# Batched attention and mixture kernel on one core: own buffers for attention outputs, merged mask pieces, condition rows in column groups, a new written order

## The reference, cut to what matters

```
ada = cond @ w_ada + b_ada                       # 6 rows of 256: shift, scale, gate, twice
x1  = mobius_add(x,  expmap(g1 * logmap(plin(attention(heads(plin(modulate(x)))))))   # 16 heads of 16, full 256 x 256 softmax
x2  = mobius_add(x1, expmap(g2 * logmap(plin(plin(modulate(x1), w_f1), w_f2))))
h   = x + (gate * local window attention(x2) + gate * attention to 64 pooled latents) @ w_out
z   = ((h * cond / 16) @ weight) * rsqrt(norm of cond * weight)
out = h + sum over the top 2 of 4 experts e: w_e * relu(z @ Wi' + (z @ A_e') @ B_e') @ Wo'
```

## Time and profile before

| | |
|---|---|
| median of 3 runs | 1249.25 us (1247.89 to 1251.9) |
| the profiled execution | 1248.74 us, its span 1246.9 us |
| mean granted TensorE clock | 0.978 |
| busy PE, DVE, ACT, POOL | 1158.8, 853.8, 706.5, 238.3 us |
| instructions | 34256 |

### The profile page before, as it was taken

One profiled execution on the slowest core, in us unless ns is written; L12 is line 12 of the kernel. 1 busy time (PEld: TensorE's weight loads), 2 busy tenths in 40 slices (PEclk: granted clock), 3 DMA queues, 4 the chain that ended last, 5 costly groups with the idle time before them and its releaser, 6 DMA issues.

```text
span 1246.9 us, 34256 instructions
## 1 busy us (share of the span) xinstructions
PE 1158.8 (93%) x13948; PEld 824.2 (66%) x13948; DVE 853.8 (68%) x3321; ACT 706.5 (57%) x1429; POOL 238.3 (19%) x336
## 2 busy tenths in 40 slices
PE   6977769999999999999999999999999999999996
PEld 2544445676667677767777677766777667777764
DVE  6858768886986857767677788767577785552332
ACT  1456676658766654757376755757465754434221
POOL 2302022022112210141113111041112120210111
PEclk9978889999999999999999999999999999999998
DMA  9220001000010100000010101000010000000000
GB/s 317 96 81 13 22 15 28 23 29 13 28 36 19 36 2 28 27 27 28 9 46 2 31 15 32 14 23 11 3 32 6 28 16 19 11 11 19 20 10 9
DMA packets 27231, 38.51 MB, mean 31 GB/s; under 512 B 3489, under 2 KB 21281, under 8 KB 27073
## 3 DMA queue, kind: packets, MB, share of 16 engines
q1 hardware_dynamic: 25280, 34.29, 8.6%
q10 hardware_dynamic: 1792, 2.03, 0.5%
HBM read 31.62 MB, written 4.29 MB: 29 GB/s over the span
## 4 chain that ended last, share of the span: by engine, by line
PE 74%; DVE 10%; ACT 9%; issue 4%; POOL 1%; DMA 1%; ACTq 0%; DVEq 0%; POOLq 0%
PE psg L436 44%; PE psq L436 16%; PE pso L436 7%; PE psg L439 7%; ACT PQ L1379 4%; DVE nm L929 2%; DMA QK<-in_w 1%; ACT QK L1379 1%; POOL M L1719 1%; ACT JA L1390 1%; DVE TU L926 1%; DVE lp L926 1%; ACT M L1379 1%; DVE JD L942 0%; DVE R L926 0%
## 5 line engine op out<-in xcount | busy, mean ns | idle before, releaser
L1379 ACT ACTIVATE PQ<-psq 128x2048 f32<-128x2048 f32 x112 | 210.2, 1877 | 86.0 <-PE psq L436 85.5
L1744 POOL TENSOR_TENSOR R<-R,rhoT 128x256 f32<-128x256 f32 x128 | 90.7, 729 | 429.0 <-ACT R L1379 429.0
L436 PE MATMUL psq<-QK 32*128 32x128 f32 (+5 forms) x3360 | 129.6, 303 | 0.2 <-DMA QK<-in_w 0.2
L436 PE MATMUL psg<-zT,WiT 128*128 128x256 f32 x512 | 123.8, 385 | 2.8 <-DVE R L926 2.7
L436 PE MATMUL pso<-PQ,Vg 128*32 128x256 f32 (+2 forms) x2048 | 111.3, 349 | 12.3 <-ACT PQ L1379 9.5
L436 PE MATMUL psg<-WoT,R 128*128 128x256 f32 x512 | 115.6, 381 | 0.0
L436 PEld LDWEIGHTS psq<-QK 32*128 32x128 f32 (+2 forms) x3360 | 93.0, 165 | 22.7 <-issue 13.7
L929 DVE TENSOR_REDUCE nm<-psq 128x16 f32<-128x2048 f32 (+1 forms) x48 | 92.7, 1931 | 21.8 <-PE psq L436 21.4
L436 PEld LDWEIGHTS psg<-zT,WiT 128*128 128x128 f32 x512 | 93.5, 192 | 18.3 <-DVE R L926 3.9
L436 PEld LDWEIGHTS psg<-WoT,R 128*128 128x128 f32 x512 | 95.2, 190 | 14.9 <-issue 2.6
L1379 ACT ACTIVATE R<-psg 128x512 f32<-128x512 f32 x64 | 38.1, 595 | 117.8 <-PE psg L436 117.6
(11 more groups left out here) (224 smaller groups left out, 2281.6 us busy)
## 6 DMA issues: line engine op xcount, KB each, us to landing
bcB<-ada_rows SPq DMA_DIRECT2D x16, 384.0 KB, 3.4
bcA<-ada_rows SPq DMA_DIRECT2D x15, 384.0 KB, 3.5
X<-in_x SPq DMA_DIRECT2D x16, 256.0 KB, 5.0
XR<-in_x SPq DMA_DIRECT2D x16, 256.0 KB, 2.7
out<-XR SPq DMA_DIRECT2D x16, 256.0 KB, 2.2
QK<-NMT SPq DMA_DIRECT2D x128, 3.0 KB
WiT<-in_WiT SPq DMA_DIRECT2D x1, 1024.0 KB, 4.9
WoT<-in_WoT SPq DMA_DIRECT2D x1, 1024.0 KB, 7.4
```

What stands on the lines that cost most here:

```text
L436: return e.matmul(o, lhsT, rhs, start=start, stop=stop, skip_group_check=True)
L1379: return e.activation(o, i, func, **kw)
L1744: e.tensor_tensor(R4, R4, rhoT[:, :], ALU.mult).then_inc(*pool_moe.mark(b, f"r{f}{j}"))
```

## The change

- O1 and OS are tiles of their own. ACT's copies of `heads(b)` wait for the last scores of batch b-1 in place of its OT.
- Local score turns: two score pieces of equal width stand side by side, and their mask is one instruction per tile with the mask row repeated. 32 mask instructions in a turn in place of 48.
- Condition rows: condT is padded to 32 columns; the three products go to partitions 0, 32 and 64 of psq[2]. DVE adds bias and the ones of the scale rows (from two new columns of hsel) in two operations of 96 partitions. The bias comes in three loads of 32 partitions. The three writes to DRAM wait for the second of these operations.
- `b1w`: 8 products in four column groups (`b1p`), an ACT copy to VB, then one product with a selecting column that sums the four groups. `b1b`: ACT squares b1 and sums along the row, then one product sums over partitions. `ff(0)` waits for the last condition row; `mix(0)` no longer does.
- hsel is loaded earlier; the written order of all five engines is new. On SP, x of batches 4 and 5 and both XR come before the late loads.

```
 "PE": [
-  "AA*AAn*qqqq*******hhn*qqqqa*naaaaaaaooohhoaqqaaqaaqaaaoonohohqNqqqFFaaaaaaaaooppopoppphhmaaaaaaaamoomNnm",
+  "A*An*qqqq****h*h**a***aanaaaaqaqooqqnohohqaqqaaqaanaahaqhooaqqaaqaoaoaaaaNhoohFFaaaoaaoaaaooppppppomomNmn",
...
 "SP": [
-  "n*****wAxwxxxAAnnN*nnNxnmNnxNnxmewNnxmNnewxmNnemwxNnxmewNnmewxNnmewNnmNewnmNewmewNmewNmNewmewmewmewee",
+  "nwxwx*****xxAAAnnN*nnNnxnmNxmNnexwnNmxNnewxmNnxmNewnxmewNnxmNewnmewNnmewNnmewNmewNmNewNmNewmewmewmewee",
...
-        O1, OS = ST1[:, 0:2], ST1[:, 2:4]
+        O1, OS = (sb(n, [128, 2, 256]) for n in ("O1", "OS"))
...
-        turns = [[(0, 0, 0), (0, 1, 192), (1, 0, 320)], [(1, 1, 0), (3, 1, 128)], [(2, 0, 0), (2, 1, 192), (3, 0, 320)]]
+        turns = [[(0, 0, 0), (1, 0, 192), (0, 1, 384)], [(1, 1, 0), (3, 1, 128)], [(2, 0, 0), (3, 0, 192), (2, 1, 384)]]
...
-                for j, o in enumerate((psq[0:16, 2, :], psq[0:16, 3, :], pso[0:16, :])):
-                    yield
-                    if j:
-                        for c in range(2):
-                            w.wait_ge(*loads[f"wada{c}1"])
-                    for c in range(2):
-                        last = mm(o, condT[:, c, :], wada[c][:, 512 * j:512 * j + 512], c == 0, c == 1)
-                    last.then_inc(*pe_ada.mark(0, f"r{j}"))
+                yield
+                for c in range(2):
+                    w.wait_ge(*loads[f"wada{c}1"])
+                for c in range(2):
+                    for j in range(3):
+                        last = mm(psq[32 * j:32 * j + 32, 2, :], condT[:, c, :], wada[c][:, 512 * j:512 * j + 512], c == 0, c == 1)
+                last.then_inc(*pe_ada.mark(0, "r"))
...
+                bank = take(pg, ("b1p",), act_late.at(0, "b1p"))
+                w.wait_ge(*loads["b1c"])
+                for h in range(2):
+                    for j in range(4):
+                        f = 4 * h + j
+                        last = mm(bank[32 * j:32 * j + 32, :], b1c[:, f:f + 1].broadcast_to([128, 32]), wx[h][:, j, :], h == 0,
+                                  h == 1)
+                last.then_inc(*pe_late.mark(0, "b1p"))
+                yield
                 bank = take(pg, ("b1w",), act_late.at(0, "b1x"))
-                w.wait_ge(*loads["b1c"])
-                for f in range(8):
-                    last = mm(bank[:, :], b1c[:, f:f + 1].broadcast_to([128, 128]), wx[f // 4][:, f % 4, :], f == 0, f == 7)
+                w.wait_ge(*loads["hsel"])
+                w.wait_ge(*act_late.at(0, "b1p"))
+                mm(bank[:, :], hsel[:, 3:4].broadcast_to([128, 128]), VB[:, :], True, True).then_inc(*pe_late.mark(0, "b1w"))
...
-                    for c, kt, q0 in turns[v]:
-                        n = 128 if kt else 192
-                        for i, j, r, o in tiles():
-                            m = 96 - 32 * j
-                            mm(psq[o, i, q0:q0 + n], unit(r), MK[r, m:m + n], q0 == 0, False)
-                    if v == 1:
-                        for i, j, r, o in tiles():
+                    n = 128 if v == 1 else 192
+                    for i, j, r, o in tiles():
+                        m = 96 - 32 * j
+                        mm(psq[o, i, 0:2 * n].rearrange("p (h n) -> p h n", h=2), unit(r),
+                           MK[r, m:m + n].unsqueeze(1).broadcast_to([32, 2, n]), True, False)
+                    for i, j, r, o in tiles():
+                        if v == 1:
                             m = 128 - 128 * (j % 2)
                             mm(psq[o, i, 256:512], unit(r), MLT[r, m:m + 256], False, False)
+                        else:
+                            m = 96 - 32 * j
+                            mm(psq[o, i, 384:512], unit(r), MK[r, m:m + 128], False, False)
...
-                for j, i in enumerate((psq[0:16, 2, :], psq[0:16, 3, :], pso[0:16, :])):
...
-                        stt(adaR[j][:, o], i[:, o], float(n in (1, 4)), bada[n // 3][0:16, k:k + 256], ALU.add,
-                            ALU.add)().then_inc(*s.mark(0, f"a{n}"))
+                for h in range(2):
+                    yield
+                    o = slice(256 * h, 256 * h + 256)
+                    w.wait_ge(*pe_ada.at(0, "r"))
+                    stt(adaR[:, o], psq[0:96, 2, o], hsel[0:96, 6 + h:7 + h], bada[1][:, o], ALU.add,
+                        ALU.add)().then_inc(*s.mark(0, f"a{h}"))
...
+                yield
+                w.wait_ge(*pe_late.at(0, "b1p"))
+                copy(VB[:, :], pg.where["b1p",][:, :]).then_inc(*s.mark(0, "b1p"))
+                e.activation(b1c, b1c, ACT.Square, accum_out=bb1[:, :]).then_inc(*s.mark(0, "b1q"))
...
                     if b:
-
-                        w.wait_ge(*pe_out.at(b - 1, "OT"))
+                        w.wait_ge(*pe_att.at(b - 1, "sc3"))
```

More of the change, by code:

```diff
@@ L47 @@
[L47 to L51, removed]
@@ L346, in program @@
         xr_in, out_done = [landing(f"d_xr{i}") for i in range(2)], [landing(f"d_out{i}") for i in range(2)]
-        pe_ada = sig("pe_ada", "bc", "r0", "r1", "r2")
-        dve_ada = sig("dve_ada", "c0", "c1", "c2", *[f"a{i}" for i in range(6)])
-        act_late = sig("act_late", "W0", "W1", "b1w", "b1x", "b1b")
+        pe_ada = sig("pe_ada", "bc", "r")
+        dve_ada = sig("dve_ada", "c0", "c1", "c2", "a0", "a1")
+        act_late = sig("act_late", "W0", "W1", "b1p", "b1q", "b1w", "b1x", "b1b")
         pool_setup = sig("pool_setup", "zero", "ones", "ident", "identb")
         pool_late = sig("pool_late", "mask", "wgkv", "gt0", "gt1", "w2sq")
-        pe_late = sig("pe_late", "W0", "W1", "b1w", "b1b", "w2sq")
+        pe_late = sig("pe_late", "W0", "W1", "b1p", "b1w", "b1b", "w2sq")
         dve_late = sig("dve_late", "gv0", "gv1", "g00", "g01", "g10", "g11", "ys", "yq", "dz", *rs("d"), "dT", "Bh", "Bl", "Bm", "Bst")
@@ L501, in late @@
                 yield
+                bank = take(pg, ("b1p",), act_late.at(0, "b1p"))
[7 more added lines that the diff above has]
+                yield
                 bank = take(pg, ("b1w",), act_late.at(0, "b1x"))
-                w.wait_ge(*loads["b1c"])
-                for f in range(8):
-                    last = mm(bank[:, :], b1c[:, f:f + 1].broadcast_to([128, 128]), wx[f // 4][:, f % 4, :], f == 0, f == 7)
-                last.then_inc(*pe_late.mark(0, "b1w"))
+                w.wait_ge(*loads["hsel"])
+                w.wait_ge(*act_late.at(0, "b1p"))
+                mm(bank[:, :], hsel[:, 3:4].broadcast_to([128, 128]), VB[:, :], True, True).then_inc(*pe_late.mark(0, "b1w"))
                 yield
                 bank = take(pg, ("b1b",), act_late.at(0, "b1b"))
-                for f in range(8):
-                    last = mm(bank[:, 0:2], b1c[:, f:f + 1].broadcast_to([128, 128]), b1c[:, f:f + 1].broadcast_to([128, 2]),
-                              f == 0, f == 7)
-                last.then_inc(*pe_late.mark(0, "b1b"))
+                w.wait_ge(*pool_setup.at(0, "ones"))
+                w.wait_ge(*act_late.at(0, "b1q"))
+                mm(bank[:, 0:2], bb1[:, :].broadcast_to([128, 128]), Vg1[:, 0, 0:2, 16], True, True
+                   ).then_inc(*pe_late.mark(0, "b1b"))
                 yield
@@ L990, in late @@
                 yq = lq[:, 3].rearrange("p (c b) -> p c b", c=2)
-                yield from chain(s, 0, ("ys", "yq"), ts(ysT[:, :, :], condT[:, :, :], 1.0 / 16, None, ALU.mult),
+                yield from chain(s, 0, ("ys", "yq"), ts(ysT[:, :, :], condT[:, :, 0:16], 1.0 / 16, None, ALU.mult),
                       tt(yq, ysT[:, :, :], ysT[:, :, :], ALU.mult))
@@ L1225, in ff @@
                         w.wait_ge(loads["adaA"][0], 32)
+                        w.wait_ge(*loads["adaB"])
                     w.wait_ge(*pe_ff.at(b, f"ug{t}"))
@@ L1282, in mix @@
                 bv = pg.where["rl", b][:, :].rearrange("p (h n) -> p h n", n=32)
-                w.wait_ge(*loads["adaB"])
                 w.wait_ge(*pe_mix.at(b, "rl"))
@@ L1401, in setup @@
                 load(e, "bqkv", bqkv[:, :], A["bqkv"].partition_broadcast(128))
-                load(e, "bada1", bada[1], A["b_ada"][768:1536].partition_broadcast(16))
+                for j in range(3):
+                    load(e, f"bada1{j}", bada[1][32 * j:32 * j + 32, :], A["b_ada"][512 * j:512 * j + 512].partition_broadcast(32))
                 load(e, "bo", bo[:, :], A["b_o"].partition_broadcast(128))
@@ L1767, in setup @@
                 load(e, "ident", ident0, A["ident"])
+                load(e, "hsel", hsel[:, :], A["hsel"])
                 load(e, "wqkv", wqkv[:, :, :], chunks("wqkv"))
@@ L1774, in setup @@
                 load(e, "w21", wx[1][:, :, 256:512], chunks("w2")[:, 4:8])
-                load(e, "hsel", hsel[:, :], A["hsel"])
                 for _ in x_load(2):
```

138 lines of the change are left out of this document (72 added, 66 removed).

## The result

The changed kernel takes 1233.49 us (median of 4 runs, 1232.33 to 1236.6) against 1248.76 us of the kernel before beside it (4 runs): ratio 0.9877, 95% interval [0.9852, 0.9902], 15.3 us less. Measured once more, as one of the second four experiments, it is 0.9858 [0.9835, 0.9881], 18.4 us less. The forecast was 20.5 less. The profiled execution took 1232.33 us with a span of 1230.2, so the spans differ by 16.7 us.

What follows compares the result with a forecast made beforehand. PE was taken to bound the kernel, save in the pipeline's filling, where batches wait on their own chains. Terms 14 + 3 + 5 - 1.5 = 20.5 us off 1248.7 gave 1228 us, range 1211 to 1242.

Steps and rivals of the forecast that it cites:

- Part 1: Condition and bias rows in the setup: column groups and fewer products save 9.3 us of PE (3.5, 4.2 and 1.6).
- Part 2: Order up to the first scores: they come at 44 us instead of 58, 14 us earlier, with DVE ending last.
- Part 3: O1/OS buffers and the filling, first scores to mixture: 3 us shorter; bounds 10 longer to 14 shorter.
- The bound of 14 us: Most the filling could shrink: 40 us of idle PE times 0.37, as missing time falls from 46 to 29.
- Part 4: Merged mask pieces, 48 to 32 instructions a turn: 0.105 us saved in each of 48 turns, 5.0 us.
- my upper bound: Most the merged masks could save: 10.1 us, if 32 instructions cost what 16 do.
- Part 5: Steady part and tail: little to gain, 13 us of tail idle stay; taken together 1.5 us lost.
- A: Rival: early start lost again because DVE and ACT set the filling, mixture only 3 us earlier; 1241 us, chance 0.17.
- B: Rival: filling shrinks 14 us and not 3, steady part keeps 2 more; 1215 us, chance 0.18.
- C: Rival: slower through the single score tile psq, 0.2 us less PE work between users adds 32 us; 1260, chance 0.07.
- D: Rival: no change, columns and not instructions price the masks, and A holds with nothing left; 1247 us, chance 0.08.
- The signs named: Trace checks: first scores at 44 (42 to 47), XR at 218, 2560 masks, 0.45 to 0.50 us a turn, steady PE 97%.

Runs made afterwards that it cites:

- second four experiments: Changed kernel again, and three variants of it or the kernel before (masks split, old order, own buffers alone), on one chip: ratios 0.9858, 0.9916, 0.9913, 1.0004.
- last experiment: Changed kernel with two letters of the written order moved, one on ACT and one on DVE: 1233.97 us, ratio 0.9867.
- second experiment: Kernel before with only the column groups for condition rows and the new bias rows; order fitted, masks and O1/OS as before: 1252.21 us, ratio 1.0001.
- third experiments: Changed kernel with the old written order, adapted only where steps fell away or came in: 1239.82 us, ratio 0.9903.

## Why the prediction was right, and where it was wrong

The direction, the size within 5 us and the range held, but by errors of opposite sign, so that the total came out near is in part luck. Against the span: start 15.9 for 14 (+1.9), filling -6.9 for +3 (-9.9), after it 7.7 for 5.0 - 1.5 (+4.2). That is 3.8 short of 20.5, the 16.7 measured.

**Part 1** held: 1.85 us for the condition rows (1.7 forecast), 2.8 for b1w (1.9 and 0.9), 0.14 for b1b. The condition rows lasted 2.10 in the second measurement and 2.95 in the last experiment, where the granted clock was lower. The square of w2c moved to 39.59 as expected, without holding anything up. That all this gives nothing in the old order was not said; the second experiment shows it.

**Part 2** held, and its numbers more closely than its sentence. "DVE, not PE, ends last there" is true of the old order once PE has less to do (3.50 us of wait in the second experiment) and half true of the new one: U came at 35.7 and not at 39, PE waited 1.53 for it and then worked without a gap until 42.01. Without that wait PE is ready at 40.5 (40 forecast).

**Part 3** is the step that failed: "I let it shrink by 3 us". The count of new PE work was right (116 to 126 us; busy time rose by 10.5). The stalls were over-valued: idle PE fell by 3.6 us and not by 13. The reasoning took a stall as removed when its place in the order was eased. But other waits took its place, which fits a chain through three engines (added work costs 9.9, 11.1 and 8.6 us for 10.2, 9.3 and 10.2). That the closing up of this chain is what ate the stalls is read from the timelines. (The bound of 14 us should be 15 by its own factors, 40 x 0.37; nothing hangs on it.) The profile also shows how the early start was spent. Batch 0's first product of ff stands at 121.54 where it stood at 121.88, although the first scores came 16 us earlier; the new order has 8 more attention steps in front of it (24 for 16). So 16 us were laid out for the other batches' attention, and 9 came back at XR. This reading rests on the timelines; no run moved batch 0 alone.

**Part 4** had the right mechanism at half its size: 0.212 us a turn (0.583 to 0.37) for 0.105. For 48 turns that is 10.2 us of PE, my upper bound. 45 turns lie behind the first XR transposes. PE's busy time there fell by 9.4 us in the old order (973.9 to 964.5) and the stretch by 7.3; in the new order, where two of three split turns hold PE 0.56 us, by 7.7 (970.8 to 963.2) and 6.9. The pair of the second and third experiments gives 9.4 (1013.6 to 1004.2), but its first value is 1.8 to 1.9 above the two other traces of the old masks in the old order. The fault was the straight line between 16 and 48 instructions: the cost of 32 is that of 16. The other price weighed there, one matmul plus 4 ns for each further tile of a pack (the Trainium skill, TensorE: Matmul & The Clock Gate, Measured speedup vs the span model), would have given 3.1 us and is further off: it had fitted the group of 16 and does not give the 0.21 us between 32 and 48.

**Part 5**: the 1.5 us of losses did not come. Behind XR the old and the new order take the same 1004 us; the added wait of ff(0) and the changes of tile shape cost nothing that shows.

**The rivals.** A (start lost, XR over 228, 1241): half of it happened. XR at 226.2 lies nearer to 228 than to my 218, and without the masks' full price the time would have been near A's. The reason given, DVE and ACT setting the filling, was nearer to the truth than my count of gaps; but 10 us more on PE cost as much. B (XR under 210) did not come: the stalls moved. C: PE's waits for PQ in front of scores grew from 10.8 to 15.2 us, 4.4 and not 32. D: columns alone don't price the masks, since with the same columns the masks alone give 0.95%.

**The signs named.** First scores within 42 to 47, yes, at its edge. XR at 218, no. 2560 mask instructions, yes; 0.45 to 0.50 us to the first score, no, 0.37. Clock of the filling over 0.88, yes, 0.90. PE at 97% in the steady part, yes. No idle of 5 us behind an Exp sequence, yes: the one of 5.88 us stands behind statistics. PE's waits for PQ past 10.8 were to prove me wrong, and they grew past it without doing so: 3.3 us of the 15.2 are one wait, at 55.71, where ACT loads the Ln table and the Exp table again (1.28 us each) between two Exps. The bound was set without a price.

## What to carry to other kernels

Before pricing an edit in a stretch where an engine is 75 to 80% busy, ask whether anything in it is covered: adding 10 us to each engine in turn tells a chain (all cost) from a bound (one does). Put the additions at more than one place, and read TensorE's busy time and granted clock beside them. As the timelines here read, in a chain a removed stall is worth only what is left when the next one has closed up, and an early start is worth what the first batch gets of it. Where the engine is full, as here behind the filling, most of the work taken off it comes back (6.9 of 7.7 us and 7.3 of 9.4), so a modest edit repeated 48 times was worth as much as the whole new order.

## What the runs showed of the hardware

**Mask packs: 32 instructions cost what 16 do, 48 cost more.** With 512 columns per tile of 32 x 32 in each case, 16 and 32 instructions hold PE 0.37 us and 48 hold it 0.58 (0.56 with pieces of 192, 192 and 128). Pieces of 384 and 128 columns cost what two of 256 do. With 256 columns per tile 32 instructions hold it only 0.27, in all 16 batches of the kernel before, so at 32 the columns still count:

```profile
1160.87 0.34 PE L436 MATMUL psq<-maskb,identb 32*32 32x128 bf16 x32
1161.14 1.13 PE L436 MATMUL psq<-QK 32*128 32x64 f32 x32
```

Why 48 cost 0.21 more was not tried.

**A late chain on DVE ran into POOL.** The first scores came at 41.7 to 43.3 us in seven executions with the new order's start, and at 46.05 in the kernel with two letters moved, both of them behind the first scores. There PE waited 2.78 us for U at 39.77. The chain was late before it met POOL: PE had waited 2.88 us for the load of w (1.75 in the changed kernel) and came back at the lower clock (0.55 between 15.9 and 22.6, where the changed kernel had 1.00 up to 20.0), and batch 0's qkv products stood at 24.80 for 22.00.

```profile
15.96 3.75 PE L437 MATMUL psq<-QK 128*128 128x512 f32 x4 [2.88 <-DMA QK<-in_w]
...
39.77 0.63 PE L440 MATMUL psg<-ident,U 128*128 128x128 f32 x4 [2.78 <-DVE U L935]
```

Just ahead of POOL's three products DVE was 2.0 us behind the changed kernel (hy at 36.10 for 34.09). DVE's timeline, then POOL's, of that kernel:

```profile
36.61 1.27 DVE L938 SCALAR_TENSOR_TENSOR hf<-hy,ha 128x96 f32<-128x96 f32 x1
37.80 1.22 DVE L935 TENSOR_TENSOR lp<-lp 128x4 f32<-128x4 f32 x1
38.94 0.68 DVE L935 TENSOR_TENSOR U<-U,hf 128x512 f32<-128x512 f32 x1
39.55 1.26 DVE L935 TENSOR_TENSOR Vg<-U,hf 128x256 f32<-128x256 f32 x1
```

```profile
36.50 2.50 POOL L1721 TENSOR_TENSOR WoT<-wat,WoT 128x512 f32<-128x512 f32 x2
38.96 1.56 POOL L1725 TENSOR_TENSOR WoT<-w2c 128x512 f32<-128x512 f32 x1
```

An operation of 4 columns that lasts 0.15 us elsewhere, one of 96 (0.26) and one of 256 (0.41) last 1.2 us here, each beside one of POOL's three products. The first two stand ahead of U and add 2.1 us to the 2.0, so U is scaled at 38.94 for 34.89. The third POOL product, begun 0.02 us after U's, lasts 1.56 for 1.03. In the second measurement of the changed kernel U was scaled from 34.43 on, before POOL began its products at 36.44, and the chain escaped. The Trainium skill (SBUF — State Buffer, Who interferes with whom) says that a VectorE instruction with two inputs in SBUF contends with a GpSimd instruction that reads SBUF, and that the contention is an exclusive lock; this trace agrees, 1.22 us for 0.15. The split into 2.0 and 2.1 us is a reading of one trace, and no run moved POOL's work.
